# Time mixing in a fused four-layer network: its weights loaded one stage earlier, and the group norm's reciprocal deviation taken by ScalarE's logarithm and exponential

## What is computed

```python
# L3: ffn (half), time mixing, ffn (half)
x = x + 0.5 * ffn(layernorm(x))
x = x + time_mix(layernorm(x))
x = x + 0.5 * ffn(layernorm(x))

# time_mix(x), H = 16 heads of K = 8
xx = shifted(x) - x
m = tanh((x + xx * maa_x) @ maa_w1)            # five low-rank corrections of 32
mw, mk, mv, mr, mg = m @ maa_w2
r, k, v = (x + xx * (maa_r + mr)) @ W_r, ... @ W_k, ... @ W_v
g = silu((x + xx * (maa_g + mg)) @ W_g)
w = time_decay + tanh((x + xx * (maa_w + mw)) @ decay_w1) @ decay_w2
S[t + 1] = S[t] * exp(-exp(w[t])) + k[t] v[t]^T    # per head, 8 x 8
y[t] = r[t] @ (S[t] + u * k[t] v[t]^T)
mu, var = mean and variance of y over each head's 8 features
yn = (y - mu) / sqrt(var + EPS) * ln_gamma + ln_beta    # EPS = 1e-5 * 64
return (yn * g) @ W_o
```

## Time and profile before

| | |
|---|---|
| Median of 3 runs | 3133.98 us (3133.33 to 3147.24) |
| Profiled execution, its own time | 3120.58 us |
| Its span, first to last instruction | 3118.8 us |
| Tensor engine busy in the span | 2330.1 us, 75% |
| Mean granted clock of the tensor engine | 0.886 |
| ffn3a, time mixing, ffn3b (start us) | about 2576, 2657, 3062 |

### The profile page before, as it was taken

How to read it: one execution, slowest core, us unless ns; L and a number is a source line. 1 busy time by engine, 2 the same in 40 slices (tenths; PEclk the granted TensorE clock), 3 DMA queues, 4 the chain that set the end, 5 groups by cost and what they waited for, 6 DMA issues and landing times. The chain is left out here.

```text
span 3118.8 us, 45117 instructions
## 1 busy us (share of the span) xinstructions
PE 2330.1 (75%) x13720; PEld 1446.9 (46%) x13720; DVE 2105.1 (67%) x5281; ACT 1459.4 (47%) x3113; POOL 920.3 (30%) x976
## 2 busy tenths in 40 slices
PE   2397689749767799899898977499575955577774
PEld 2397477648634122222222235389365954122223
DVE  3465788746544799999998824466674666587785
ACT  2265311126443388888887842166323653123222
POOL 4644235534413200000100004534274431131230
PEclk9999799869888699999999987699777977798987
DMA  4122100012211300000000000022211220000000
GB/s 143 43 66 67 40 8 15 18 34 63 79 34 34 128 19 20 19 19 18 19 19 17 7 29 25 30 61 62 59 40 44 64 86 0 23 0 0 0 0 28
DMA packets 112250, 115.54 MB, mean 37 GB/s; under 512 B 22064, under 2 KB 95504, under 8 KB 111248
## 3 DMA queue, kind: packets, MB, share of 16 engines
q1 hardware_dynamic: 93136, 71.44, 8.2%
q0 software_dynamic: 17408, 35.95, 3.4%
q10 hardware_dynamic: 1472, 5.27, 0.5%
HBM read 67.36 MB, written 44.83 MB: 36 GB/s over the span
## 5 line engine op out<-in xcount | busy, mean ns | idle before, releaser
L1732 DVE TENSOR_REDUCE attn_mx<-bank 128x1 f32<-128x512 f32 x1024 | 640.8, 682 | 61.0 <-PE bank L1511 52.8
L1633 ACT ACTIVATE attn_pT<-bank 128x512 f32<-128x512 f32 x1024 | 539.8, 604 | 126.7 <-PE bank L1526 126.3
L1511 PE MATMUL bank<-attn_K,attn_Q 48*128 48x512 bf16 x1024 | 336.4, 396 | 50.4 <-DVE attn_mx L1732 29.9
L1526 PE MATMUL bank<-attn_Q,attn_K 51*128 51x512 bf16 x1024 | 331.0, 386 | 2.5 <-ACT attn_pT L1633 1.4
L1539 PE MATMUL bank<-attn_pT,attn_vb 128*32 128x512 f32 x2048 | 276.2, 611 | 19.9 <-ACT attn_pT L1633 11.8
L1692 POOL TENSOR_TENSOR attn_m_rem<-attn_m_rem,attn_m_parts 8x128 f32<-8x128 f32 x128 | 53.3, 416 | 678.5 <-ACT attn_m_parts L1646 678.5
L1511 PEld LDWEIGHTS bank<-attn_K,attn_Q 48*128 48x128 bf16 x1024 | 71.8, 94 | 376.0 <-DVE attn_mx L1732 325.2
L2380 POOL TENSOR_TENSOR mix_rS<-mix_rT,mix_S 128x512 f32<-128x512 f32 x64 | 81.5, 1278 | 288.7 <-ACT mix_gT L2360 228.0
L903 PE MATMUL bank<-mix_prod_qk,ident 128*128 128x256 f32 x512 | 121.5, 392 | 0.0
L903 PEld LDWEIGHTS bank<-mix_prod_qk,ident 128*128 128x128 f32 x512 | 101.2, 199 | 25.2 <-issue 11.8
L2316 PE MATMUL bank<-mix_rS,mix_sel 128*128 128x512 f32 x128 | 73.8, 664 | 43.0 <-POOL mix_rS L2380 43.0
(11 more groups left out here) (610 smaller groups left out, 5927.3 us busy)
## 6 DMA issues: line engine op xcount, KB each, us to landing
ffn0a_x_ring<-xs_rows SPq DMA_DIRECT2D x72, 65.0 KB, 1.8
ffn0b_x_ring<-xs_rows SPq DMA_DIRECT2D x72, 65.0 KB, 1.8
ffn2a_x_ring<-xs_rows SPq DMA_DIRECT2D x72, 65.0 KB, 1.8
ffn2b_x_ring<-xs_rows SPq DMA_DIRECT2D x72, 65.0 KB, 1.8
w<-in_L_w ACTq DMA_DIRECT2D x2, 2048.0 KB, 16.3
ffn0a_y_back<-y_rows SPq DMA_DIRECT2D x8, 512.0 KB
ffn0b_y_back<-y_rows SPq DMA_DIRECT2D x8, 512.0 KB
w<-in_L_w SPq DMA_DIRECT2D x2, 2048.0 KB, 10.7
```

The costliest lines, as they stand in the source:

```text
L1511: nc.tensor.matmul(a_bank[n % 3][:], slot(net.Q, h, 0, KROWS)[:, qt * P:(qt + 1) * P], slot(net.K, h, 0, KROWS)[:, hf * CH:(hf + 1) * CH], ...
L1526: nc.tensor.matmul(s_bank[n % 3][:], slot(net.K, h, 0, KROWS + MROWS)[:, kt * P:(kt + 1) * P], slot(net.Q, h, 0, KROWS + MROWS)[:, hf * CH ...
L1633: nc.scalar.activation(pT[:, kt % RING, hf * CH:(hf + 1) * CH], s_bank[(n * HPB + hf) % 3][:], ACT.Exp, scale=HD ** -0.5).then_inc(exp_rea ...
L1732: nc.vector.tensor_reduce(mx[:, h % 2, qt, hf:hf + 1], a_bank[n % 3][:], AX.X, ALU.max).then_inc(a_used, 1)
```

## The change

The weights of time mixing become an object of their own, allocated ahead of `ffn3a`. `ffn3a` gets it as `later` and issues its loads on SyncE; `time_mix_stage` only waits for them. The host lays `w2` out with its zeros (`L3_w2a`) and `v_rep` with the partition first, so that there are 16 transfers in place of 26, and GpSimd's fill of `w2a` goes.

The deviation and its reciprocal, a square root on ScalarE and a reciprocal on VectorE, become a logarithm and an exponential on ScalarE: rstd = exp(-0.5 * ln(var + EPS)). ScalarE's step has two waits more, for the buffer `rstd` to be free (`yg_ready`) and for its own logarithm (`log_ready`).

```diff
+class TimeMixWeights:
+
+    def __init__(self, nc, net, part):
+        self.net = net
...
+        self.loads = part.sem("time_mix_weights_loaded")
+        self.mats = [(self.W[k], "L3_" + k) for k in self.W] + [
+            (self.w1, "L3_w1"), (self.dw1, "L3_dw1"), (self.dw2, "L3_dw2"), (self.sel, "sel"), (self.vecs, "L3_vecs"),
+            (self.w2a, "L3_w2a"), (self.w2b, "L3_w2b"), (self.Wv_rep, "L3_v_rep")]
+
+    def load(self, sp):
+        for t, name in self.mats:
+            sp.dma_start(t[:], self.net.ins[name]).then_inc(self.loads, 16)
+
+    def wait(self, eng):
+        eng.wait_ge(self.loads, 16 * len(self.mats))
...
-def rwkv_ffn_stage(nc, net, tag, src, dest):
+def rwkv_ffn_stage(nc, net, tag, src, dest, later=None):
...
         block = st.block()
+
+        if later:
+            @block.sync
+            def _(sp):
+                later.load(sp)
...
-def time_mix_stage(nc, net, tag, src, dest):
+def time_mix_stage(nc, net, tag, src, dest, weights):
...
-        @block.sync
-        def _(sp):
-            for t, name in mats:
-                sp.dma_start(t[:], net.ins[name]).then_inc(loads, 16)
-            sp.wait_ge(setup, 1)
-            for f in range(4):
-                sp.dma_start(w2a[f * TM:(f + 1) * TM, f, :], net.ins["L3_w2"][f]).then_inc(loads, 16)
-            sp.dma_start(w2b[:], net.ins["L3_w2"][4]).then_inc(loads, 16)
-            for j in range(HD):
-                sp.dma_start(Wv_rep[:, j, :], net.ins["L3_v_rep"][j]).then_inc(loads, 16)
-            sp.wait_ge(loads, 16 * NLOAD)
...
-            pe.wait_ge(loads, 16 * NLOAD)
+            weights.wait(pe)
...
-            act.wait_ge(loads, 16 * NLOAD)
-            act.wait_ge(setup, 2)
+            weights.wait(act)
+            act.wait_ge(setup, 1)
...
             def deviation(c):
                 act.wait_ge(var_ready, c + 1)
-                nc.scalar.activation(std[:], var_bank[:], ACT.Sqrt, bias=gn_eps[:]).then_inc(std_ready, 1)
+                nc.scalar.activation(log_var[:], var_bank[:], ACT.Ln, bias=gn_eps[:]).then_inc(log_ready, 1)
+                need(act, yg_ready, c)
+                act.wait_ge(log_ready, c + 1)
+                nc.scalar.activation(rstd[:], log_var[:], ACT.Exp, scale=-0.5).then_inc(rstd_ready, 1)
...
-            nc.gpsimd.memset(w2a[:], 0.0).then_inc(setup, 1)
             nc.gpsimd.memset(gn_eps[:], GN_EPS).then_inc(setup, 1)
...
-            dve.wait_ge(loads, 16 * NLOAD)
+            weights.wait(dve)
...
             def group(c):
-                steps = Chain(dve, gn_step, c * 3)
+                steps = Chain(dve, gn_step, c * 2)
                 dve.wait_ge(yc_kept, c + 1)
-                dve.wait_ge(std_ready, c + 1)
-                steps.then(nc.vector.reciprocal(rstd[:], std[:]))
-                steps.wait()
+                dve.wait_ge(rstd_ready, c + 1)
                 steps.then(nc.vector.tensor_tensor(yn[:], yc[:], rstd[:], ALU.mult))
...
-                  lambda s, d: rwkv_ffn_stage(nc, net, "ffn3a", s, d),
-                  lambda s, d: time_mix_stage(nc, net, "mix3", s, d),
+                  lambda s, d: rwkv_ffn_stage(nc, net, "ffn3a", s, d, last),
+                  lambda s, d: time_mix_stage(nc, net, "mix3", s, d, last),
...
             if n == 9:
                 experts.close()
+                last = TimeMixWeights(nc, net, Part(nc, st.enter_context(Scope(nc)), "mix3"))
...
-    a["L3_v_rep"] = np.stack([np.repeat(g["L3_attn_W_v"][:, j::HD], HD, axis=1) for j in range(HD)])
-    a["L3_w1"], a["L3_w2"] = g["L3_attn_time_maa_w1"], g["L3_attn_time_maa_w2"]
+    a["L3_v_rep"] = np.stack([np.repeat(g["L3_attn_W_v"][:, j::HD], HD, axis=1) for j in range(HD)], axis=1)
+    a["L3_w1"], w2 = g["L3_attn_time_maa_w1"], g["L3_attn_time_maa_w2"]
+    a["L3_w2a"], a["L3_w2b"] = np.zeros((P, 4, D), np.float32), w2[4]
+    for f in range(4):
+        a["L3_w2a"][f * TM:(f + 1) * TM, f] = w2[f]
```

More of the change, by code:

```diff
@@ L2185 @@
 GN_EPS = 1e-5 * HD ** 2
-def time_mix_stage(nc, net, tag, src, dest):
+class TimeMixWeights:
+    def __init__(self, nc, net, part):
+        self.net = net
+        self.w2a, self.w2b = part.sb("w2a", [P, 4, D]), part.sb("w2b", [TM, D])
+        self.sel = part.sb("sel", [P, HD, D])
+        self.W = {k: part.sb(f"W{k}", [P, D]) for k in ("r", "k", "v", "g", "o", "blockones", "center", "blockmean")}
+        self.w1 = part.sb("w1", [P, NMIX * TM])
+        self.dw1, self.dw2 = part.sb("dw1", [P, TD]), part.sb("dw2", [TD, D])
+        self.Wv_rep = part.sb("Wv_rep", [P, HD, D])
+        self.vecs = part.sb("vecs", [P, 10])
+        self.loads = part.sem("time_mix_weights_loaded")
[8 more added lines that the diff above has]
+def time_mix_stage(nc, net, tag, src, dest, weights):
     with Scope(nc) as st:
@@ L2208, in time_mix_stage @@
         rs = part.sb("rS", [P, 4, CH])
-        rku, bonus, y, yc, sq, std, rstd = (part.sb(k, [P, CH])
-                                            for k in ("rku", "bonus", "y", "yc", "sq", "std", "rstd"))
+        rku, bonus, y, yc, sq, log_var, rstd = (part.sb(k, [P, CH])
+                                            for k in ("rku", "bonus", "y", "yc", "sq", "log_var", "rstd"))
         yn, yg = part.sb("yn", [P, CH]), part.sb("yg", [P, CH])
-        w2a, w2b = part.sb("w2a", [P, 4, D]), part.sb("w2b", [TM, D])
@@ L2213, in time_mix_stage @@
-        sel = part.sb("sel", [P, HD, D])
         gn_eps = part.sb("gn_eps", [P, 1])
[L2215 to L2220, removed]
+        w2a, w2b, sel, W_, w1 = weights.w2a, weights.w2b, weights.sel, weights.W, weights.w1
@@ L2221, in time_mix_stage @@
+        dw1, dw2, Wv_rep, vecs = weights.dw1, weights.dw2, weights.Wv_rep, weights.vecs
+        (setup, xx_ready, m_ready, m_kept, mix_ready, mix_used, mixed, lin_ready, lin_kept, w1_ready, w1_kept,
          w2_ready, wd_ready, e1_ready, rep_ready, kv_done, scanned, rs_ready, y_acc, rku_ready, bonus_ready,
          bonus_used) = (part.sem(k) for k in (
-             "loads", "setup", "xx_ready", "m_ready", "m_kept", "mix_ready", "mix_used", "mixed", "lin_ready", "lin_kept",
+             "setup", "xx_ready", "m_ready", "m_kept", "mix_ready", "mix_used", "mixed", "lin_ready", "lin_kept",
@@ L2224, in time_mix_stage @@
              "w1_ready", "w1_kept", "w2_ready", "wd_ready", "e1_ready", "rep_ready", "kv_done", "scanned", "rs_ready",
              "y_acc", "rku_ready", "bonus_ready", "bonus_used"))
-        (y_whole, yc_ready, yc_kept, sq_ready, var_ready, std_ready, yg_ready, out_ready, out_added, own) = (
-            part.sem(k) for k in ("y_whole", "yc_ready", "yc_kept", "sq_ready", "var_ready", "std_ready",
+        (y_whole, yc_ready, yc_kept, sq_ready, var_ready, log_ready, rstd_ready, yg_ready, out_ready, out_added, own) = (
+            part.sem(k) for k in ("y_whole", "yc_ready", "yc_kept", "sq_ready", "var_ready", "log_ready", "rstd_ready",
@@ L2232, in time_mix_stage @@
         vec = {k: vecs[:, i:i + 1] for i, k in enumerate(names)}
-        mats = [(W_[k], "L3_" + k) for k in W_] + [(w1, "L3_w1"), (dw1, "L3_dw1"), (dw2, "L3_dw2"), (sel, "sel"),
-                                                    (vecs, "L3_vecs")]
-        NLOAD = len(mats) + 4 + 1 + HD
         block = st.block()
```

## The result

The changed kernel takes 3114.66 us in the median of 5 runs (3103.95 to 3119.57) against 3140.26 for the kernel before in the same session. The ratio is 0.9923, with a 95% interval of 0.9897 to 0.9949: 24 us faster, between 16 and 32. The forecast was 21.7 us less, and 3112.3 us for the time.

The account below looks back on a forecast made before the run. No engine was full (tensor engine busiest, 75%); time saved on time mixing's own path shortens the span. Pause 14.0 + seven chunks 6.2 + last chunk 1.45 = 21.7 us; 3133.98 - 21.7 = 3112.3 us, range 3104 to 3122.

Parts of the forecast that it names:

- The pause: Entry into time mixing behind ffn3a: with weights loaded early, VectorE starts 0.34 us after ffn3a's last copy, saving 14.0 us.
- The slow exit of 2.28 us: Barrier leaving ffn3a: if its block's DMAs make the exit that slow, early weights save only 12.1 us.
- The yn step: Group norm: a 1.28 us table load between logarithm and exponential; yn starts 2.04 us after the logarithm, VectorE gains 1.44.
- The last chunk: Group norm at time mixing's end, with no products in between: 1.45 us saved, all on the path to ffn3b.
- The seven chunks: Group norm of chunks 0 to 6: each gains the smaller of 1.44 us and tensor engine idle time, 6.21 us together.
- the room ahead of the projection: Tensor engine idle time before the projection in seven chunks: 0.26 to 1.57 us each, 6.38 us together, limiting the gain.
- Chunk 0: First 512-token chunk of time mixing: the sum had no term for a change in its length.
- A: Group norm: one table serves logarithm and exponential, no second load; sum 23.1 us, time 3110.9; chance 0.15.
- B: The group norm gives next to nothing, by later rstd or tensor engine clock; time 3119.5, or 3120 to 3122; chance 0.20.
- C: All of time mixing: tensor engine clock stays near half level, making the kernel slower, 3150 us or more; chance 0.03.

Follow-up runs that it names:

- whole_b: The whole change measured once more against the kernel before: ratio 0.9912 (0.9896 to 0.9928), 27 us faster.
- gn_only: Kernel before with only the new logarithm and exponential group norm, weights still loaded in the stage: ratio 0.9967 to the kernel before, 10.3 us faster.
- whole: The whole change measured again, beside its parts on the same chip, against the kernel before: ratio 0.9941 (0.9923 to 0.9960), 18.4 us faster.
- one_table: The whole change plus an explicit load, ahead of the logarithm's wait, of the table holding logarithm and exponential: ratio 0.9906 to the kernel before, 3088.2 us.

## Why the prediction was right

The sum was 14.0 + 6.2 + 1.45 = 21.7 us; the three timed comparisons of the whole change give 24, 18 and 27 us, the profiles 19.3 to 20.3 over the end of the kernel. That they agree so well with 21.7 is in part luck: the seven chunks gave 1.0 to 1.8 us more than forecast, and the one profile of before that they are compared with has the short chunk 0, which takes 3 us off.

- **The pause.** 14.0 forecast, 14.0 measured: VectorE starts 0.33 us behind ffn3a's last copy, with 0.34 forecast. The slow exit of 2.28 us, the low bound, didn't come; that ffn3a's block now issues DMAs doesn't slow its exit.
- **The yn step.** A load before the exponential, yn 2.04 us behind the logarithm's end: as worked out. The Trainium skill (ScalarE: Activation LUTs, What ACT_TABLE_LOAD costs) counts a further 1.38 us of drain with a switch. The trace doesn't agree: the load starts 0.01 us behind the logarithm's end and the exponential 0.02 us behind its load.
- **The last chunk.** 1.45 forecast, 1.4 measured in two profiles of the whole change. In whole_b and gn_only it was 0.7 and 0.8, because there the mean-removing product at its start ran at the half level for a while, 1.83 and 1.73 us in place of 1.12; the reciprocal's part is the same.
- **The seven chunks.** The mechanism held: VectorE and the tensor engine arrive at the projection almost together. The size was off: 6.2 us forecast, 7.2 to 8.0 measured. The mis-sized term is the room ahead of the projection, which I took from the idle time in the trace of before. Three of its seven chunks had k, r and v wholly at the half level, and I gave them 0.26 us each. That idle time counts from the end of the last v pass in the records. At this level such a record is 1.06 us long, but the passes follow each other every 0.85 us, so the projection could move by 0.47 us. whole_b shows it. It too has three chunks of this kind, and in each the projection starts 5.28 us behind k, 0.85 us behind the last v pass. Before, it was 5.75 us, as the earlier trace rows has it. The second of the seven:

```profile
2752.61 2.08 PE L2302 MATMUL bank<-mix_x_mixed,mix_Wk 128*128 128x512 f32 x2 [2.49 <-DVE mix_x_mixed L2432]
...
2757.89 1.16 PE L2278 MATMUL bank<-mix_Wo,mix_yg 128*128 128x128 f32 x8
```

  In whole_b's four other chunks the projection starts 1.38 to 1.45 us sooner than before. Three times 0.47 and these four make 7.0 us. Two chunks of before also had a slower projection there (1.35 us in the earlier trace rows and 1.33, against 1.16 here), which cost them 0.19 and 0.17 us more. The sum is 7.4 us, and whole_b's seven chunks gained 7.4.

  The granted clock over k, r and v also changes from profile to profile. In the changed kernel's first profile only one chunk had it wholly at the half level. These are the fourth and the fifth of the seven:

```profile
2872.70:2877.10 4.40, 4.37 (x7) 0.63 0.00 0
2918.30:2923.70 5.40, 5.40 (x7) 0.50 0.00 0
```

  There the stretch from k to the first replicated product became shorter in six chunks by 1.0 to 1.6 us, in the fifth by 0.45, 8.7 in all; the scans behind it took 0.6 us more. In which chunks the clock is low isn't a property of the kernel's order that can be carried over. It moves the sum little: with one, one, two and three such chunks (the first profile, whole, gn_only, whole_b) the gain was 8.0, 7.5, 7.2 and 7.4 us.
- **Chunk 0.** I had it unchanged. It took 3 us more in the profile, because the clock rose later, and hid what the seven chunks gave above the forecast. As gn_only and one_table show, this isn't a cost of the change but a scatter that a sum from one profile can't foresee.
- **The rivals.** A, one table for both, was wrong for this kernel and right in its price once made: 1.3 us in the last chunk; in the seven others 0.7 to 2.8 us, not clear of their scatter, where I had 0.2. B and C didn't come: the group norm gave 9.4 us in the profile, and the mean clock over the seven chunks is 0.92 in both.

## What to carry to other kernels

A load that a stage waits for at its entry is worth its whole pause if another stage without transfers runs ahead of it; the price is one object that both stages know. When an engine's work is shortened in the middle of a chain, look at who else stands in front of the next step: here the reciprocal's 1.44 us paid because the tensor engine had about as much room in most chunks, the next 1.28 us paid a third at most, and moving one product in the tensor engine's order came with as much as the whole group norm had given. Take the room from the starts of the instructions ahead, not from the ends of pipelined records: that was 0.26 against 0.47 us here. Stages ahead of a change can differ by 20 us between two executions, so compare the stretch, not the span.

## What the hardware showed beyond that

- The tensor engine's clock at this stage's entry: after the pause it works at the half level (1.2 GHz) first. For the same instructions the full level came 5.4 and 5.8 us behind VectorE's first instruction in two profiles and 7.1 to 8.4 us behind it in seven. Between the two patterns chunk 0 differs by 3 us. My expectations put the early rise at 6 and the late one at 8 to 9, by windows of 1 us; they are a little too late.
- At the half level the two passes of a 128x512 float32 product start 0.85 us apart, while their records are 1.06 us long; at the full level it is 0.43 and 0.59 us.
- The length of the part ahead of ffn3a, which neither the change nor an experiment touches, was 2567 to 2596 us in twelve profiles.
- An explicitly loaded table serves both logarithm and exponential: 0.03 us between them in place of 1.31.
